# x1 through DRAM as 32 padded rows instead of 128: one store in 512-byte pieces, three loads in 8,320-byte rows

## What is computed

```
x = x + attention(mixed(x, cond))          # a 32x32 channel mix per sample, 32 heads of 16, signs of the weights
y = conv1d(x, width 9, pad 4, 4 groups of 8 channels) + context(cond) + bias
x = x + moe(y)                             # router over 8 experts, top 2, rank 16, down to 512
```

## Time and profile before

| | before |
|---|---|
| median of 3 runs | 136.77 us (136.05 to 140.3) |
| the profiled execution | 136.54 us |
| its span in the trace | 134.7 us |
| granted TensorE clock, mean | 0.974 |
| busy: PE, DVE, ACT, POOL | 85%, 70%, 47%, 36% |
| issues of x1 to DRAM (L274) | 8 x 256 KB, median 4.9 us from issue to landing |
| issues of windows (L280) | 24 x 256 KB, median 4.5 us |

### The profile page before, as it was taken

How to read it: one execution, slowest core, us unless ns; L and a number is a source line. 1 busy time by engine, 2 the same in 40 slices (tenths; PEclk the granted TensorE clock), 3 DMA queues, 4 the chain that set the end, 5 groups by cost and what they waited for, 6 DMA issues and landing times. The chain is left out here.

```text
span 134.7 us, 2543 instructions
## 1 busy us (share of the span) xinstructions
PE 114.7 (85%) x876; PEld 89.4 (66%) x876; DVE 93.9 (70%) x251; ACT 63.6 (47%) x139; POOL 48.1 (36%) x58
## 2 busy tenths in 40 slices
PE   1389999695799997899799999999999669967970
PEld 1269699694697996698698876767676329543720
DVE  0073999629795987999588797797456555395862
ACT  4629889964233688362637355364331202230320
POOL 1117000001605693366579989674330030000000
PEclk9999999999779999999999999999999995999999
DMA  3999999500000000001852924919392949496123
GB/s 65 276 363 421 400 412 409 215 6 2 0 5 0 0 0 0 5 2 78 158 80 90 211 88 100 208 53 221 120 207 67 216 127 208 134 223 242 78 100 133
DMA packets 18317, 19.27 MB, mean 143 GB/s; under 512 B 960, under 2 KB 14080, under 8 KB 17920
## 3 DMA queue, kind: packets, MB, share of 16 engines
q1 hardware_dynamic: 18304, 19.11, 51.6%
HBM read 14.91 MB, written 4.19 MB: 142 GB/s over the span
## 5 line engine op out<-in xcount | busy, mean ns | idle before, releaser
L360 POOL TENSOR_TENSOR probs<-probs,row_inv 128x512 f32<-128x512 f32 x16 | 16.7, 1049 | 17.2 <-DVE row_inv L864 17.2
L1216 PE MATMUL bank<-mixed_hi,qkv_sign 128*128 128x256 f32 x72 | 18.1, 293 | 1.2 <-DVE scale_v L746 1.2
L1217 PE MATMUL bank<-mixed_lo,qkv_sign 128*128 128x256 f32 x72 | 17.3, 282 | 0.0
L366 POOL TENSOR_TENSOR x_all<-x_all,o_out 128x512 f32<-128x512 f32 x8 | 10.2, 1278 | 13.8 <-DVE o_out L878 13.8
L1216 PEld LDWEIGHTS bank<-mixed_hi,qkv_sign 128*128 128x128 f32 x72 | 14.0, 194 | 1.5 <-DVE scale_v L746 1.3
L1294 PE MATMUL bank<-wo_sign,attn_hi 128*128 128x512 f32 x32 | 13.4, 418 | 1.3 <-DVE attn_lo L869 1.3
L1217 PEld LDWEIGHTS bank<-mixed_lo,qkv_sign 128*128 128x128 f32 x72 | 13.9, 194 | 0.0
L507 ACT ACTIVATE probsT<-bank 128x512 f32<-128x512 f32 x16 | 9.6, 597 | 7.7 <-PE bank L1270 7.5
L501 ACT ACTIVATE probs<-probs 128x512 f32<-128x512 f32 x16 | 9.9, 628 | 6.9 <-DVE probs L854 6.9
L1294 PE MATMUL bank<-wo_sign,attn_lo 128*128 128x512 f32 x32 | 12.6, 393 | 0.0
L1258 PE MATMUL bank<-keys_diag,queries 64*128 64x128 f32 x128 | 9.5, 288 | 3.6 <-issue 2.6
(11 more groups left out here) (141 smaller groups left out, 232.1 us busy)
## 6 DMA issues: line engine op xcount, KB each, us to landing
rows_sb<-x_turned SPq DMA_DIRECT2D x24, 256.0 KB, 4.5
x_all<-in_x_rows SPq DMA_DIRECT2D x4, 512.0 KB, 9.3
x_turned<-x_all SPq DMA_DIRECT2D x8, 256.0 KB, 4.9
out_rows<-x_all SPq DMA_DIRECT2D x8, 256.0 KB, 2.6
qkvT_sb<-in_qkvT SPq DMA_DIRECT2D x4, 384.0 KB, 6.4
rows_sb<-in_qkv_rows SPq DMA_DIRECT2D x1, 1536.0 KB, 10.5
rows_sb<-in_wo_rows SPq DMA_DIRECT2D x1, 1024.0 KB, 13.3
woT_sb<-in_woT SPq DMA_DIRECT2D x1, 1024.0 KB, 15.8
```

The costliest lines, as they stand in the source:

```text
L360: pool.tensor_tensor(probs[:, t % 2, h, :, :], probs[:, t % 2, h, :, :], row_inv[:, t % 2, h, :].unsqueeze(2).to_broadcast([P, HALF, TOKENS]),
L366: pool.tensor_tensor(x1[:, t, :], x_all[:, t, :], o_out[:, t % 2, :], ALU.add).then_inc(x1_ready, 1)
L1216: mm(dst, w, mixed_hi[:, ph, cols(i % 2, PAIR)], start=(ph == 0 and n % 2 == 0), stop=False)
L1217: last = mm(dst, w, mixed_lo[:, ph, cols(i % 2, PAIR)], start=False, stop=(ph == PHASES - 1 and n % 2 == 1))
```

## The change

x1 no longer goes to DRAM as it lies. There are two DRAM tensors, one per window buffer, each holding 32 rows (channel in its group, phase) of 2,080 elements, the shape that a window has, and 2 elements more. The store of a tile writes its 512 runs of 128 elements at element 1 of each run of 130. The borders of the runs are zeros in DRAM: POOL sets the whole first 32 partitions of both window buffers to zero, and four DMAs (`clear_pads`) copy them to DRAM before the first tile. A window then comes back as three loads of 32 whole rows of 2,080 elements (8,320 bytes), the load of shift n starting n elements further on; the border zeros come with them. The convolution reads its steps from element 0 of each run instead of 1. The store of tile t also waits until the loads of tile t-2 have landed, and the semaphore of the loads is now one per buffer.

```diff
-        x1_dram = nc.dram_tensor("x1_turned", (ROWS, HIDDEN), F32, kind="Internal").ap()
+        win_rows = [nc.dram_tensor(f"x1_rows{n}", (TOKENS * win_w + 2,), F32, kind="Internal").ap() for n in range(2)]
...
+            def clear_pads():
+                sp.wait_ge(win_cleared, 2)
+                for n in range(2):
+                    sp.dma_start(win_rows[n][0:TOKENS * win_w].rearrange("(p w) -> p w", w=win_w),
+                                 x1_win[n][0:TOKENS].rearrange("p s g m -> p (s g m)")).then_inc(pads_cleared, 16)
+                    sp.dma_start(win_rows[n][TOKENS * win_w:].rearrange("(p w) -> p w", p=1),
+                                 x1_win[n][0:1, 0, 0, 0:2]).then_inc(pads_cleared, 16)
+                sp.wait_ge(pads_cleared, 64)
+
             def to_window(t):
-                rows = x1_dram[t * P:(t + 1) * P, :]
+                rows = win_rows[t % 2]
+                runs = rows[0:TOKENS * win_w].rearrange("(cp sg m) -> sg cp m", cp=TOKENS, m=STEPS + 2)
                 sp.wait_ge(x1_ready, t + 1)
-                sp.dma_start(rows, x1[:, t, :]).then_inc(x1_stored, 16)
+                reached(sp, windowed[t % 2], 48 * (t // 2))
+                sp.dma_start(runs[:, :, 1:1 + STEPS], x1[:, t, :]).then_inc(x1_stored, 16)
                 sp.wait_ge(x1_stored, 16 * (t + 1))
-                if t == 0:
-                    sp.wait_ge(win_cleared, 4)
                 reached(sp, conv_done, t - 1)
                 for shift in range(3):
-                    sp.dma_start(x1_win[t % 2][TOKENS * shift:TOKENS * (shift + 1), :, :, 2 - shift:2 - shift + STEPS]
-                                 .rearrange("p s g m -> p (s g) m"),
-                                 rows.rearrange("(sg c) (ph m) -> (c ph) sg m", c=MEMBERS_IN, m=STEPS)
-                                 ).then_inc(windowed, 16)
+                    sp.dma_start(x1_win[t % 2][TOKENS * shift:TOKENS * (shift + 1), :, :, :].rearrange("p s g m -> p (s g m)"),
+                                 rows[shift:shift + TOKENS * win_w].rearrange("(p w) -> p w", w=win_w)).then_inc(windowed[t % 2], 16)
...
+            clear_pads()
             for t in range(TILES):
                 to_window(t)
...
                 for n in range(2):
-                    pool.memset(x1_win[n][0:TOKENS, :, :, 1:2], 0.0).then_inc(win_cleared, 1)
-                    pool.wait_ge(win_cleared, 2 * n + 1)
-                    pool.memset(x1_win[n][2 * TOKENS:WINDOW, :, :, STEPS:STEPS + 1], 0.0).then_inc(win_cleared, 1)
-                    pool.wait_ge(win_cleared, 2 * n + 2)
+                    pool.memset(x1_win[n][0:TOKENS, :, :, :], 0.0).then_inc(win_cleared, 1)
...
-                pe.wait_ge(windowed, 16 * 3 * (t + 1))
+                pe.wait_ge(windowed[t % 2], 48 * (t // 2 + 1))
...
-                              x1_win[t % 2][:, :, g, 1:1 + STEPS], start=True, stop=True)
+                              x1_win[t % 2][:, :, g, 0:STEPS], start=True, stop=True)
```

More of the change, by code:

```diff
@@ L189, in build @@
         ones_ready, quad_ready, sums_cleared = sem("ones_ready"), sem("quad_ready"), sem("sums_cleared")
-        win_cleared, table_ready = sem("win_cleared"), sem("table_ready")
+        win_cleared, pads_cleared, table_ready = sem("win_cleared"), sem("pads_cleared"), sem("table_ready")
         cond_done, cond_gelu = sem("cond_done"), sem("cond_gelu")
@@ L222, in build @@
         x1_stored = sem("x1_stored")
-        windowed, conv_done, conv_biased = sem("windowed"), sem("conv_done"), sem("conv_biased")
+        windowed = [sem(f"windowed{n}") for n in range(2)]
+        conv_done, conv_biased = sem("conv_done"), sem("conv_biased")
         convT_done, convT_copied = sem("convT_done"), sem("convT_copied")
```

## The result

The changed kernel is slower: 142.98 us (median of 4 runs, 142.47 to 146.91) against 136.41 us for the kernel before beside it (136.04 to 140.3), ratio 1.051, 95% interval 1.040 to 1.062. Forecast were 138.2 us and a range that ended at 140.8, so the direction was right and the size was not. Some executions of every kernel here are slower as a whole, and the ratios leave those out. The profiled execution is the slowest of its kind, 146.91 us; its start phase, up to the first MEMSET of the windows, is 2.9 us longer than before's. Nothing in the change stands there: PE starts the `mix` ahead of `score(0)` at 32.75 us, in e2, e4, e8 and e11, which keep the change's instructions up to there, at 29.7 to 30.0, and in e5, a form of the kernel before, at 32.76. So I leave the start phase out and compare stages.

A forecast was written before the change was run, and what follows sets the result against it. PE, busy 85%, was taken to bound the kernel, with gaps behind POOL's list and late windows. 136.54 + 2.7 (MEMSETs) - 1.0 (late gaps) = 138.2 us; range 134.0 to 140.8, the forecast's own 136.7 to 139.6.

The forecast's parts named there:

- Part 1: POOL's two wide MEMSETs ahead of keys_diag: score(0) 2.9 us later, taken as a 2.7 us loss with the clock.
- Part 2: clear_pads' four DMAs on SP and the store's wait for the loads of tile t-2: cost nothing.
- Part 3: Window loads into 32 partitions: long rows run at 208 GB/s, 3.8 us, a window complete 0.4 us sooner.
- Rival 1: Long-row loads run at the input loads' rate, 400 GB/s, taking 2.0 us: 134.2 us in all; chance 0.18.
- part 5: Late PE gaps ahead of convolve(5) and convolve(7): SP rounds of 6.5 us, convolve(7) earlier, gain 1.0 us.
- Part 4: Store of x1 in 512 pieces starting 4 bytes in: 1.2 us for its data, 0.5 us more than before.
- Rival 2: Odd-address store slow: from 0.8 us more, windows 7 come later; 1.4 more gives 142.0 us, 2.3 more 146.5; chance 0.15.

The follow-up runs named there:

- e2: Changed kernel with clear_windows moved behind spread_keys(1) in POOL's list, so no MEMSET stands ahead of a keys_diag; 140.25 us, ratio 1.015.
- e4: Changed kernel with the store of before, 128 rows of 2,048 bytes (result left wrong); 138.43 us, ratio 1.016.
- e8: e4 with each load brought to 128 partitions x 520 elements instead of 32 x 2,080, same bytes (result left wrong); 135.39 us, one run.
- e11: e2 with SP's list reordered: stores of tiles 3 to 6 ahead of the loads of the tile before; 139.7 us, ratio 1.023.
- e5: e3 with x1 stored in 512 pieces at a pitch of 128 elements, aligned, loads keeping their piece size; 139.63 us, one run.
- e1: Kernel before with its two small MEMSETs of the first 32 partitions widened from 16 to 2,080 elements, DMAs as before; 141.45 us, ratio 1.029.
- e12: e2 with one more wait, so its two MEMSETs start only when DVE's scale chain is through; 137.78 us, ratio 0.999.
- e3: Kernel before with clear_windows moved behind spread_keys(1) in POOL's list; 134.25 us.
- e9: e3 repeated in more rounds for an interval; 134.1 us, ratio 0.969.
- e10: e3 with SP's list reordered: stores of tiles 3 to 6 ahead of the loads of the tile before; 131.6 us, ratio 0.956.
- e7: e2 with runs of 144 elements, x1 from element 16, so each store piece starts at a multiple of 64 bytes; 139.53 us, ratio 1.022.
- e6: e3 with x1 stored in 512 pieces at a pitch of 130 elements, each starting 4 bytes in; 144.73 us, one run.

## Why the prediction was wrong

**Part 1, the MEMSETs: right, the clock beside it a little low.** 1.8 us each was forecast, 1.82 measured; 5.5 us of idle PE, 5.44 measured; e1 shows that nothing absorbs it. For the clock I took 0.2 us off, 2.7 in all. The longer rest brought 6.8 us of 1.2 GHz instead of 3.4, and how much of it PE had to work in differs from run to run. Up to `convolve(3)`, rest and work together, e8 loses 3.2 us, e4 3.3 and e1 3.5, all within the 1.9 to 3.6 that I had written down; the profiled execution of the change, with 6.0 us worked at the low clock, loses 2.8 + 1.3 = 4.1. The term is mis-sized by 0.5 to 0.8 us, and by 1.4 in that one execution. (The upper bound of part 1 took 2.0 ns an element from `keys_diag`; the earlier trace rows give 2.4. Nothing rests on it.)

**Part 2: right.** clear_pads ran at 39 us, beside nothing that waits; the wait for tile t-2 cost nothing in this order (e11 shows where it would).

**Part 3, the loads: right.** 4.4 to 4.8 us for the last load was forecast, 4.8 measured at tile 0 and 4.7 at tiles 6 and 7; e8 shows that the cause, 32 partitions, was the right one. Rival 1 is out. The worth was right too. With nothing added for the store, part 5's own arithmetic has rounds of 6.0 us, the loads of tile 7 at 114.0 and convolve(7) 2.0 us earlier; e4, with the old store, gives 2.1.

**Part 4, the store: the step that failed.** I added 0.5 us for it; it is 2.0 us alone, and 0.6 to 1.4 us in each of the last two full rounds (6.8 and 7.2 us in the changed kernel, 7.5 and 7.3 in e2, against 6.1 and 5.9 in e4). The rate of unheld 512-byte pieces was read off a transfer from DRAM into SBUF, 281 GB/s, and taken for one in the other direction, which no row of before showed. Measured, such a store runs at 175 GB/s. With aligned pieces it needs 1.1 us more than one of 2 KB rows, and the 4 bytes another 0.9, between the last byte and the landing, where the sum had no term.

**Part 5: failed with part 4.** Rounds of 6.5 us were forecast and are about 7.2. Convolve(7) was to come 1.0 us earlier against convolve(3), and comes 1.6 later, or 2.8 to 4.9 later where the early stage is undisturbed (e12, e2). The sentence that the low clock behind the late gap would go fell with it: that gap grew. The last stage, from convolve(7) on, is 1.9 us longer in the profiled run for a low stretch at 131.7 us behind the wait for window 7; e1 has one at 126.7 us and a last stage of 14.1 us with before's DMAs, so this part belongs to no edit alone.

With what the profiled execution shows the sum is +2.8 (MEMSETs) + 1.3 (clock) + 1.6 (rounds) = 5.7 us, and 1.9 for the last stage; the medians differ by 6.6. How the other three executions divide the 6.6 is not known. Against the forecast, the first two terms are off by 0.5 to 1.4 us and the rounds by 2.6, so the rounds, and with them the store, carry most of the miss.

Rival 2 had this mechanism and its turning point (0.8 us). That its 142.0 us lies near 142.98 is in part luck: it stands for a store 1.4 us slower, and with the 2.0 us measured alone the same arithmetic gives 145.0, since a round does not become longer by all of them. It had 15% where the unknown direction of the transfer deserved more.

## What to carry to other kernels

Turning data through DRAM costs pieces on one side or the other: price the store and the load each from a transfer of that direction, piece size and alignment, from issue to landing and not by the rate alone, and treat a rate read in the other direction as no evidence. In a loop store, wait, load, wait on one queue, the price that counts is the landing of the store behind the loads, so first try the order of the queue (1.9 to 2.8 us from e3 and e9 to e10, where the long loads had given 2.1 in e4). Work that prepares something for much later should not stand ahead of an item on the path in an in-order list: one call moved, `clear_windows()`, was worth about 4 us to the kernel before (ratio 0.969).

## What the hardware showed that I had not expected

- A MEMSET of 32 x 2,080 elements on POOL held a DVE TENSOR_SCALAR of 4 elements a row for 3.10 us (e2) and 3.25 us (the changed kernel) instead of 0.15; it ended when the second of the two MEMSETs did. In e7, where the MEMSETs are 32 x 2,304, it was held for 1.65 us and ended with the first. The TENSOR_REDUCE and TENSOR_TENSOR of 128x512 that ran beside the MEMSETs in e12 kept their usual 0.6 to 0.7 us. The Trainium skill ("SBUF — State Buffer", "Who interferes with whom") says that a DVE instruction in a 2-port mode, for which TENSOR_SCALAR is named, is blocked whole by GpSimd; the trace agrees, and adds that of two MEMSETs back to back it can be held for one or for both.
- Longer rests of PE went with longer stretches at 1.2 GHz. Rests of 5.43 to 6.02 us (e4, e8, the changed kernel, e1), of 4.32 (e2) and of 3.69 (e5) had 6.8 us of it, one of 7.24 (e6) had 10.2. Rests of 2.13 and 2.61 us in the kernel before had 3.4 us each, but one of 1.91 there and those of 2.02 and 2.19 in e9 had none. Part of such a stretch can pass while PE still rests.
- A store of 256 KB in 512-byte pieces that start 4 bytes off lands 1.3 us after its last byte has moved (e6, the changed kernel), one of aligned pieces or of whole rows 0.4 us after it (e5, before).
- Long rows did not make the loads issue much faster: three take 1.24 us on SP instead of 1.36.
